# Routing weights that travel with the token rows: multiplied in the experts stage instead of in combine

## What is computed

```python
x = x + tanh(g_xattn) * attention(layernorm(x), ctx)        # 128 x 64 = 8192 tokens of 128 values
h = layernorm(x)
probs = softmax(h @ router_w + router_b)                    # E = 8
topk_p, topk_i = top_k(probs, 2)
topk_p = topk_p / sum(topk_p)                               # the two routing weights of a token
moe = sum_k topk_p[k] * expert[topk_i[k]](h)                # gelu((h @ w1 + b1) * gate) @ w2 + b2
y = moe + shared_expert(h) * sigmoid(shared_weight)
x = x + tanh(g_ffn) * (layernorm(y) * ln_g + ln_b)
```

## Time and profile before

| | us |
|---|---|
| median of 3 runs | 1027.6 (1027.29 to 1041.74) |
| the profiled execution | 1027.21 |
| its span, first to last instruction | 1025.4 |
| PE busy in the span | 721.9 (70%) |
| DVE | 741.0 (72%) |
| ACT | 554.5 (54%) |
| POOL | 601.7 (59%) |

### The profile page before, as it was taken

The page is one execution under the profiler, slowest core; times in us unless marked ns, Lnnn a source line. Parts: engine busy times, 40 slices in busy tenths (PEclk is TensorE's granted clock), DMA queues, the critical chain, the costliest instruction groups (busy, mean ns, idle before and its releaser), DMA issues. The chain is left out here.

```text
span 1025.4 us, 26459 instructions
## 1 busy us (share of the span) xinstructions
PE 721.9 (70%) x7850; PEld 570.9 (56%) x7851; DVE 741.0 (72%) x2078; ACT 554.5 (54%) x1131; POOL 601.7 (59%) x658
## 2 busy tenths in 40 slices
PE   2888778788777788777535899998888888850000
PEld 1556555555555555555424788888888888740000
DVE  5699999988999999889653975444444444436997
ACT  2777656677666677655212345555555554526553
POOL 5454666756666757665518904666666666650544
PEclk9899999999999999998856899999999999985555
DMA  4211222122212123000107201222222222215442
GB/s 119 50 38 47 59 54 61 35 66 62 63 50 59 34 67 84 28 15 30 42 31 228 65 3 52 62 61 60 62 62 62 59 62 57 62 53 153 127 119 82
DMA packets 91301, 66.19 MB, mean 65 GB/s; under 512 B 17009, under 2 KB 80753, under 8 KB 91249
## 3 DMA queue, kind: packets, MB, share of 16 engines
q1 hardware_dynamic: 70048, 35.49, 13.8%
q0 software_dynamic: 8448, 17.45, 5.4%
q10 hardware_dynamic: 12752, 12.58, 3.6%
HBM read 38.21 MB, written 23.09 MB: 60 GB/s over the span
## 5 line engine op out<-in xcount | busy, mean ns | idle before, releaser
L834 POOL TENSOR_TENSOR prob<-prob,mx 128x1024 f32<-128x1024 f32 x64 | 121.6, 1900 | 148.5 <-DVE mx L536 148.4
L1286 POOL DMA_INDIRECT expert_results<-y,dest x136 | 148.7, 1093 | 82.7 <-POOL dest L1282 56.2
L1100 ACT ACTIVATE hT<-bank,b1g_c,gate_c 128x256 f32<-128x256 f32 x272 | 138.1, 558 | 88.2 <-issue 38.5
L166 POOL DMA_INDIRECT expert_lists<-xn,slots x128 | 125.0, 977 | 66.9 <-issue 30.6
L1041 PE MATMUL bank<-w,hT 128*128 x1088 | 139.6, 281 | 24.1 <-ACT hT L1100 20.2
L1041 PEld LDWEIGHTS bank<-w,hT 128*128 128x128 f32 x1088 | 127.2, 191 | 39.2 <-issue 39.2
L366 PE MATMUL bank<-kbd,qg 128*64 128x256 f32 x1024 | 136.6, 407 | 4.6 <-DVE prob L529 2.0
L762 ACT ACTIVATE PT<-bank 128x512 f32<-128x512 f32 x128 | 70.1, 592 | 81.4 <-PE bank L377 80.4
L383 PE MATMUL bank<-w_att,aT 128*128 128x128 f32 x128 | 33.5, 347 | 94.0 <-issue 62.5
L529 DVE TENSOR_TENSOR prob<-bank,mask 128x512 f32<-128x512 f32 x128 | 86.0, 673 | 18.6 <-PE bank L366 14.0
L366 PEld LDWEIGHTS bank<-kbd,qg 128*64 128x64 f32 x1024 | 71.0, 145 | 45.3 <-issue 16.3
(11 more groups left out here) (182 smaller groups left out, 1743.3 us busy)
## 6 DMA issues: line engine op xcount, KB each, us to landing
rows<-expert_lists SPq DMA_DIRECT2D x70, 130.0 KB
yin<-expert_results SPq DMA_DIRECT2D x16, 512.0 KB, 5.3
x_all<-in_x SPq DMA_DIRECT2D x16, 256.0 KB
ctx_in<-in_ctx SPq DMA_DIRECT2D x16, 256.0 KB
pad_k<-in_mask_BxS_ik SPq DMA_DIRECT2D x16, 256.0 KB
xn2T<-x2T ACTq DMA_DIRECT2D x16, 256.0 KB
out<-res ACTq DMA_DIRECT2D x7, 512.0 KB, 3.2
expert_results<-y,dest POOLq DMA_INDIRECT x136
```

Source lines behind the costliest of these rows:

```text
L166: po.indirect_dma_start(lists[:, :], bass.IndirectOffsetOnAxis(ap=m.slots[:, par, t, k:k + 1], axis=0), m.xn2[:, par, t, :], None).then_in ...
L834: po.tensor_tensor(ps, ps, mx[:, u, :].unsqueeze(2).broadcast_to([P, H, S]), ALU.subtract).then_inc(subbed, 1)
L1100: ac.activation(hT[:, par, c, :], h_ps[par][c // 2][:, (c % 2) * SL:(c % 2 + 1) * SL], ACT.Gelu, bias=b1g_c[:, c, bass.ds(e, 1)], scale=ga ...
L1286: po.indirect_dma_start(results[:, :], bass.IndirectOffsetOnAxis(ap=dest[:, par, h, :], axis=0), y[:, par, h, :], None).then_inc(sent[par] ...
```

## The change

A row gets two more values, so `ROW = D + 4`: the first weight minus the second (column D + 2), and the second weight (column D + 3). `route_b` writes them into the row, and the tile `weight` is gone. Since pad rows have zeros there, their weight is zero.

In the experts stage `meta` has four columns. POOL's comparison gives 1 where the step's expert is the token's first, and 0 elsewhere (`share`). From it come as before the destination, and now also the weight: share * (w1 - w2) + w2. DVE multiplies `y` by `share` into a new tile `yw`, and POOL sends `yw`. The semaphores are counted anew: `placed` has 6 increments a step; `y_taken` says that `y` has left PSUM, `y_ready` that `yw` is there. DVE's wait on the earlier sends (`sent`) now stands between `y` and `yw`. `take_meta` and ACT's `b2_now` wait for the whole of `place`, with the cast.

In combine `weigh` and DVE's product are gone: DVE adds the two results (`both`), then the shared expert's (`acc`). All 14 steps of the norm of group g - 1 stand behind the statistics of group g, and ACT scales group g, not g - 2, in its body g.

The diff, cut to its core:

```diff
-ROW = D + 2
+ROW = D + 4
...
-RB_STEPS = 5
+RB_STEPS = 6
...
-                p2, s2 = r_m[:, 4], r_m[:, 5]
-                tiles = bass.ds(q * QT, QT)
+                p2, s2, w2nd = r_m[:, 4], r_m[:, 5], r_m[:, 0]
...
-                    ve.tensor_copy(weight[:, tiles, 0], s2)
-                    ve.tensor_tensor(weight[:, tiles, 1], p2, s2, ALU.mult)
+                    ve.tensor_tensor(w2nd, p2, s2, ALU.mult).then_inc(rb_step, 1)
...
                 elif i == 6:
                     need(ve, xn2_ready, q, per=QT, total=NQ)
+                    need(ve, rb_step, q, per=RB_STEPS, k=4, total=NQ, apart=True)
                     ve.tensor_scalar(xn2[:, par, :, D], r_m[:, 1], -1.0, float(E), ALU.mult, ALU.add)
+                    ve.tensor_tensor(xn2[:, par, :, D + 2], s2, w2nd, ALU.subtract)
+                    ve.tensor_copy(xn2[:, par, :, D + 3], w2nd)
                     ve.tensor_copy(xn2[:, par, :, D + 1], cst[:, bass.ds(q * QT + C_TOKEN, QT)])
...
-                    pe.wait_ge(y_ready, t - 1)
+                    pe.wait_ge(y_taken, t - 1)
...
-                            ac.wait_ge(y_ready, t - 1)
-                            wait_apart(ac, destf_step, t * 2 - 2)
+                            ac.wait_ge(y_taken, t - 1)
+                            wait_apart(ac, placed, t * PLACED - PLACED)
...
-                    ve.wait_ge(destf_step, (t - 1) * 2)
+                    ve.wait_ge(placed, (t - 1) * PLACED)
...
                 ve.wait_ge(b2_ready, t + 1)
+                ve.wait_ge(y_done, t + 1)
+                ve.tensor_tensor(y[:, par], y_ps[par][:, 0:2 * D].rearrange("p (h d) -> p h d", d=D),
+                                 b2_now[:, par, 0:D].unsqueeze(1).broadcast_to([P, 2, D]), ALU.add).then_inc(y_taken, 1)
                 if not isinstance(i, int) or i >= 1:
                     ve.wait_ge(sent[par], i * 32)
-                ve.wait_ge(y_done, t + 1)
-                ve.tensor_tensor(y[:, par], y_ps[par][:, 0:2 * D].rearrange("p (h d) -> p h d", d=D),
-                                 b2_now[:, par, 0:D].unsqueeze(1).broadcast_to([P, 2, D]), ALU.add).then_inc(y_ready, 1)
+                wait_apart(ve, placed, t * PLACED + 5)
+                ve.wait_ge(y_taken, t + 1)
+                ve.tensor_tensor(yw[:, par], y[:, par], share[:, par].unsqueeze(2).broadcast_to([P, 2, D]),
+                                 ALU.mult).then_inc(y_ready, 1)
                 take_meta(t + 2, par, i + 1)
...
-            def place(t, par):
+            def place(t, par, i):
 
                 po.wait_ge(meta_read, t + 1)
                 if not isinstance(t, int) or t >= 2:
-                    po.wait_ge(dest_ready, t - 1)
+                    po.wait_ge(y_ready, t - 1)
                 wait_apart(po, b2_ready, t + 1)
-                po.tensor_scalar(destf[:, par], meta[:, par, :, 0], b2_now[:, par, D:D + 1], -float(TOK),
-                                 ALU.is_equal, ALU.mult).then_inc(destf_step, 1)
-                po.wait_ge(destf_step, t * 2 + 1)
-                po.tensor_tensor(destf[:, par], destf[:, par], meta[:, par, :, 1], ALU.add).then_inc(destf_step, 1)
-
-            def body(t, par, i):
-                place(t, par)
+                po.tensor_scalar(share[:, par], meta[:, par, :, 0], b2_now[:, par, D:D + 1], None,
+                                 ALU.is_equal).then_inc(placed, 1)
+                wait_apart(po, placed, t * PLACED + 1)
+                po.tensor_scalar(destf[:, par], share[:, par], -float(TOK), None, ALU.mult).then_inc(placed, 1)
+                po.wait_ge(placed, t * PLACED + 2)
+                po.tensor_tensor(share[:, par], share[:, par], meta[:, par, :, 2], ALU.mult).then_inc(placed, 1)
+                po.tensor_tensor(destf[:, par], destf[:, par], meta[:, par, :, 1], ALU.add).then_inc(placed, 1)
+                po.wait_ge(placed, t * PLACED + 4)
+                po.tensor_tensor(share[:, par], share[:, par], meta[:, par, :, 3], ALU.add).then_inc(placed, 1)
                 if not isinstance(i, int) or i >= 1:
                     po.wait_ge(sent[par], i * 32)
-                wait_apart(po, destf_step, t * 2 + 2)
-                po.tensor_copy(dest[:, par, :, 0], destf[:, par]).then_inc(dest_ready, 1)
-                po.wait_ge(dest_ready, t + 1)
+                wait_apart(po, placed, t * PLACED + 5)
+                po.tensor_copy(dest[:, par, :, 0], destf[:, par]).then_inc(placed, 1)
+
+            def body(t, par, i):
+                place(t, par, i)
+                wait_apart(po, placed, t * PLACED + PLACED)
                 wait_apart(po, y_ready, t + 1)
                 for h in range(2):
                     po.indirect_dma_start(results[:, :], bass.IndirectOffsetOnAxis(ap=dest[:, par, h, :], axis=0),
-                                          y[:, par, h, :], None).then_inc(sent[par], 16)
+                                          yw[:, par, h, :], None).then_inc(sent[par], 16)
...
                 if later(g):
-                    sp.wait_ge(acc_step, (g - 1) * A_STEPS)
+                    sp.wait_ge(acc_step, (g - 1) * 2)
...
-                if i == 0:
-                    ve.tensor_tensor(first[:, par, 0:H], yin[:, par, 0, 0:H],
-                                     weight[:, bass.ds(g * GT, H), 0:1].broadcast_to([P, H, D]),
-                                     ALU.mult).then_inc(acc_step, 1)
-                elif i == 1:
-                    ve.wait_ge(acc_step, g * A_STEPS + 1)
-                    ve.wait_ge(weighed, g * W_STEPS + W_STEPS)
-                    ve.tensor_tensor(first[:, par], first[:, par],
-                                     shared[:, bass.ds(g * GW, GW)].rearrange("p (t d) -> p t d", d=D),
-                                     ALU.add).then_inc(acc_step, 1)
-                else:
-                    ve.wait_ge(acc_step, g * A_STEPS + 2)
-                    if later(g):
-                        ve.wait_ge(scaled, (g - 1) * GT)
-                    ve.tensor_tensor(acc[:, par], first[:, par], second[:, par], ALU.add).then_inc(acc_step, 1)
+                ve.wait_ge(y_in[par], i * 32 + 32)
+                if later(g) or g == 1:
+                    wait_apart(ve, acc_step, g * 2)
+                ve.tensor_tensor(both[:, :, :], yin[:, par, 0], yin[:, par, 1], ALU.add).then_inc(acc_step, 1)
+                if later(g):
+                    ve.wait_ge(scaled, (g - 1) * GT)
+                wait_apart(ve, acc_step, g * 2 + 1)
+                ve.tensor_tensor(acc[:, par], both[:, :, :],
+                                 shared[:, bass.ds(g * GW, GW)].rearrange("p (t d) -> p t d", d=D),
+                                 ALU.add).then_inc(acc_step, 1)
 
             def stats(g, par, t):
                 if t == 0:
-                    wait_apart(ve, acc_step, g * A_STEPS + A_STEPS)
+                    wait_apart(ve, acc_step, g * 2 + 2)
                 ve.bn_stats(st[:, par, t, :], acc[:, par, t, :]).then_inc(stat_step, 1)
...
-            BEHIND_ADD = ((0, 1), (2, 3), (4,))
-            BEHIND_STATS = ((5,), (6, 7), (8,), (9, 10), (11,), (12, 13), (), ())
+            BEHIND_STATS = ((0, 1), (2, 3), (4, 5), (6, 7), (8, 9), (10, 11), (12,), (13,))
 
             def body(g, par, i):
-                ve.wait_ge(y_in[par], i * 32 + 32)
-                chained = later(g) or g == 1
-                for k in range(A_STEPS):
-                    add(g, par, k)
-                    if chained:
-                        for step in BEHIND_ADD[k]:
-                            norm(step, g - 1, 1 - par)
+                add(g, par, i)
                 for t in range(GT):
                     stats(g, par, t)
-                    if chained:
+                    if later(g) or g == 1:
                         for step in BEHIND_STATS[t]:
...
-            def weigh(g, par, i):
-                wait_apart(ac, y_in[par], i * 32 + 32)
-                if later(g):
-                    wait_apart(ac, acc_step, (g - 1) * A_STEPS)
-                for k, t in [(0, t) for t in range(H, GT)] + [(1, t) for t in range(GT)]:
-                    w = weight[:, bass.ds(g * GT + t, 1), :].rearrange("p a k -> p (a k)")
-                    ac.activation((first, second)[k][:, par, t, :], yin[:, par, k, t, :], ACT.Copy, scale=w[:, k:k + 1])\
-                      .then_inc(weighed, 1)
...
-                weigh(g, par, i)
-                if later(g):
-                    scale(g - 2, par)
-                if later(g) and not (isinstance(g, int) and g < 3):
-                    store(g - 3, 1 - par)
-            groups(ac, body, pairs=2)
-            scale(NGR - 2, 0)
-            store(NGR - 3, 1)
-            scale(NGR - 1, 1)
-            store(NGR - 2, 0)
+                scale(g, par)
+                if later(g) or g == 1:
+                    store(g - 1, 1 - par)
+            groups(ac, body)
```

26 lines of the change are left out of this document (13 added, 13 removed).

## The result

The changed kernel took 1105.97 us in the median of four executions (1103.54 to 1106.41), against 1027.76 for the kernel before: a ratio of 1.0721, interval 1.0629 to 1.0812. The ratio compares the means, and one of the four executions of the kernel before took 1041.74 us; by the medians it is 1.0761. Forecast were 1108 and a range of 1074 to 1148. The profiled execution is the shortest of the four; the median stands 2.4 us higher.

A forecast was written before the change was run, and what follows sets the result against it. POOL's chain from send to send was taken to pace the experts stage: 1027.2 + 82.5 (1.25 us a step, 66 steps) + 3 (attention) - 5 (combine) = 1107.7, say 1108 us; range 1074 to 1148.

The forecast's parts named there:

- The three new instructions: Experts stage: POOL's two products and one addition, with their gaps, add 0.95 us a step, bounds 0.7 and 1.3.
- The weighting and the contention: Experts stage: `yw` on VectorE delays POOL's send by 0.30 us a step, bounds 0.1 and 0.5.
- my two candidates: Experts stage, send's delay from `yw`: 0.21 us by waiting for it alone, 0.40 if `yw` holds the cast.
- rival A: Experts stage: the 0.84 us before send 1 absorbs POOL's new instructions; step stays 4.35, total 1025 us; 2%.
- Attention: Attention stage: one more tiny operation and a fulfilled wait per quad, 16 quads; +3 us, bounds 1 and 10.
- Combine: Combine stage: first scaling 4.4 us earlier, tail 1 us shorter, group unchanged at 11.4; -5 us, bounds -12 and 0.
- they fill that hole and don't lengthen the circle: Combine: 2.1 us of VectorE instructions replace L1400's standstill for POOL; the repeating group path `acc`, chain, scaling stays 11.4 us.
- PE's own pace: Experts stage: PE needs 3.93 us a step when nothing holds it, leaving 1.67 of 5.60 to spare.
- B: Experts stage: PE drops to its lower clock; 1260 us if for good, likelier +10 to +30 us; 6%, 1% for all.
- C: Experts stage: `yw` holds the cast and weight copy L1216 falls into both sends; 1.8 us a step, 1144 us; 12%.
- D: Experts stage: the additions are cheap, 0.8 us a step, 53 us in all, total 1078 us; 12%.
- E: Combine: the circle shrinks as ScalarE's multiplications were in it; -12 us, total 1101; near variant within the forecast's 68%.

The follow-up runs named there:

- the last two kernels: Place on VectorE in the kernel before, weights and combine unchanged: 958.64 us; changed kernel with place on VectorE and four norm steps ahead, run again: 960.09 us.
- The experiment with four steps ahead: Changed kernel with the norm's first four steps of the earlier group between combine's two additions: 1088.95 us, ratio 1.0717.

## Why the prediction was right, and where its terms were off

The ground was right: POOL's chain from send to send sets the step, nothing covers what is put into it. The single added instruction shows it (0.355 us a step, 23 us in the kernel), and so does the opposite, POOL's instructions taken away.

That the total came within 2 us of the median is in part luck. Against the profiled execution, which the forecast was built on, it is 4.2 us high: the experts stage was 5.7 too high and attention 3.9, combine 5.4 too low.

*The three new instructions*: taken 0.95, measured 0.83. A one-input instruction on 128x2 took 0.22 where I took 0.25, the wait in front of it 0.19 where I took 0.17; and L1285 started 0.15 behind the start of L1284, before that had ended, so the pair costs less than two. From the start of L1284 to that of L1287 are 0.43 us.

*The weighting and the contention*: taken 0.30, measured 0.27 by removing it, 0.26 on the cast. Of my two candidates the dependency alone (0.21) would have shown a send 0.84 behind `yw` and a cast of 0.19; the trace has the cast at 0.45 and the send 0.91 behind it and 0.96 behind `yw`. The hold was right but shorter than the 0.40 I gave it: I had let the cast run its full 0.19 behind the end of `yw`, and it ended 0.05 behind it. The two candidates lie closer together than I thought: by the estimate above the dependency alone would have given 0.15, so more than half of the 0.27 would be there without any hold, and no run has the one without the other in the order of the changed kernel. The rule of the Trainium skill ("SBUF — State Buffer", Who interferes with whom) on two SBUF inputs on VectorE agrees with all three cases here, cast held by 0.26, addition held by 0.16, and neither without `yw`.

*Not in the sum*: the pause before the first send grew from 0.84 to 0.91 with one more separate wait in front of it, 4.6 us over the stage. It is 0.91 without `yw` too, and with `share` on VectorE, so it goes with the wait and not with the new instructions. A 0.84 that has changed its size was one of my signs of being wrong; it grew by 0.07, where rival A would have it shrink. Together the step is 1.13 longer, not 1.25. The 66 steps make 74.9 of the stage's 76.8 us; the rest stands in the first step and behind the last comparison, which my sum left out.

*Attention*, +3: the first pair of traces has -0.9 up to the experts stage. On two other chips the same distance can be read where a kernel with the old attention ran beside one with the new. The first copy of meta starts at 603.79 (one more instruction on POOL) against 607.64 (the changed kernel) and 605.36 (place on VectorE), and at 602.13 against 606.88 (the last two kernels). So +1.6 to +4.8 there, with single executions, of which those of four kernels with the same attention on one chip differ by 1.3 us; what hid it in the first pair stays open. Where POOL's hold went can be read from the groups of VectorE after, 20 to 500 us:

```profile
L664 DVE COPY xn<-cst 128x4 f32 (+1 forms) x13 | 24.5, 1887 | 0.0
...
L662 DVE TENSOR_TENSOR xn<-r_m 128x4 f32<-128x4 f32 x13 | 2.1, 159 | 0.0
L667 DVE CAST slots<-slotf 128x8 int32<-128x8 f32 x13 | 2.0, 155 | 0.0
```

The cast is free (155 ns instead of the 1688 of the earlier trace rows) and the copy in front of it has the hold, not the subtraction that I named.

*Combine*, -5: this is the term that failed, and the step of it is "they fill that hole and don't lengthen the circle". The first scaling did come 4.5 us earlier (11.4 us behind the first addition, forecast 11.5), but the circle grew from 11.4 to 11.95. What I put in the hole was not all free to run there: statistics and aggregations ran beside POOL's L1478 at 0.30 and 0.64, but L1398, the next of the chain, was held and took 1.00. The Trainium skill (the same section) counts `tensor_scalar`, the kind of L1398, with one input, among those that can take the ports shared with GpSimd; the row agrees, and I had applied its rule to instructions with two inputs alone. From the end of `acc` (1045.44) to the start of step 4, L1405 at 1048.25, are 2.8 us instead of my 2.1, and the hold's 0.83 (1.00 less 0.17) covers the difference. In all the chain behind `acc` takes 1050.55 - 1045.44 = 5.1 us until L1411 ends, where it took 988.01 - 983.57 = 4.4. Over six groups the longer circle gives back 3.3 us. The first addition, too, came 9.9 us behind the last send (1003.56 - 993.63), where the first multiplication had come 9.2 behind it (926.91 - 917.75). With -4.5 that is -0.5; the last 1.0 lies in the tail. From the start of the last addition into `acc` to the end are 23.6 us instead of 22.6, in all five profiles with this combine, where I had forecast 1 us less: the last chain was held as well (L1398 took 1.08 us at 1082.42). The experiment with four steps ahead restores a group of 11.2 and 5.4 us.

*PE's own pace*: I read 3.93 from one pair of first layers and called it PE's pace "when nothing holds it". It was no bound of PE: the pauses ahead of the second layer (61 us in the stage) go when POOL's chain goes, and PE then takes 3.5. For the forecast it did not matter, since 5.5 is above both. It would have mattered for the question what a change of the opposite kind could gain: 66 x 0.43 = 28 us more than I would have said.

*Rivals*: that POOL absorbs the instructions (A) is excluded by the single instruction, which cost 0.355 of the 0.41 expected. The clock stayed at 0.99 (B). The weight copy did fall into more sends than before, 131 of 136 instead of 100 (C), but only with a part of its length: the 33 sends that had nearly all of it beside them took 1.32 us before, and after the change a step's first send takes 1.04 and its second 1.11 on the mean, together no more than before. The cheap additions (D) lay 0.33 a step under what was measured. The circle did not shrink (E).

## What to carry to other kernels

When one engine's instruction chain from send to send adds up to the step with nothing left over, price every tiny instruction put there at its duration plus the gap in front of it (0.36 us here, for two numbers a partition), and look for the engine that waits on that chain: here it had the time to do the work itself. The chain that a change lengthens is also the one to shorten: with the place moved off GpSimd the kernel before became 5.5% shorter, and the changed one, with its norm ahead, ended at the same time. When an instruction moves next to another engine's long one, ask which kind of instruction will be issued then, not how many.

## What the runs showed of the hardware

- The pause between POOL's own cast and an indirect send on POOL was 0.84 us with one separate wait and 0.91 with two. Where VectorE released the send, it started 0.80 to 0.86 behind the end of `y` or `yw` (623.82 - 622.97 at the head of the changed kernel, 795.83 - 795.02 with the place on VectorE). The 0.95 to 1.10 in the brackets of such sends are POOL's idle time since its last send, not this pause. It runs from the last release: with `y` ready early it is 0.91 behind the cast.
- On POOL a product with a constant on 128x2 took 0.22, a two-input instruction 0.20, the cast 0.19, a comparison with a value from SBUF 0.30; on VectorE the comparison took 0.23 and the addition 0.16. The gaps behind them, 0.08 to 0.19, count nearly as much.
- POOL and VectorE held each other until the running instruction was through, in three pairs: 0.19 became 0.45 and 0.20 became 0.36 next to a 0.42 `yw`, 0.17 became 1.00 next to the end of a 3.01 addition, and each ended 0.03 to 0.06 behind the instruction that held it. Statistics, with one input, ran at 0.30 beside the same addition (0.28 elsewhere).
- With PE busy in 162 of 220 us (620 to 840) in the changed kernel and in 220 of 220 with the place on VectorE, the granted clock was 1.00 both times.
